# Four edits to an attention and gated-FFN kernel on 8 cores: no casting pre-pass, a layer norm emitted behind the first FFN block, fewer PSUM banks in the projections, an earlier evacuation

## The reference

```python
xn = layernorm(x)                                   # x: [16, 2048, 1024] f32
q, k, v = heads(xn @ Wq + bq), heads(xn @ Wk + bk), heads(xn @ Wv + bv)   # 16 heads of 64
att = softmax(causal(q @ k.T / 8))
y = (att @ v) @ Wo + bo
s = (y - mean(y)) * rsqrt(var(y) + 1e-5) * gamma + beta
wg, wu, wd = w_gate / 127, w_up / 127, w_down / 127  # int32 weights, hidden size 3072
g = silu((silu(xn @ wg.T) * (xn @ wu.T)) @ wd.T)
out = x + s * g
```

## Time and profile before

| what | value |
|---|---|
| median of the 2 runs | 7192.64 us (7139.81 and 7245.48) |
| time of the profiled execution | 7139.81 us |
| its span, slowest core (core 1) | 7138.2 us |
| spans of the 8 cores | 7108.4 to 7138.2 us |
| busy: PE, DVE, ACT, POOL | 81%, 19%, 24%, 1% of the span |
| mean granted TensorE clock | 0.886 on both dies |

### The profile page before, as it was taken

One profiled execution on the slowest core, in us unless ns is written; L12 is line 12 of the kernel. 1 busy time (PEld: TensorE's weight loads), 2 busy tenths in 40 slices (PEclk: granted clock), 3 DMA queues, 4 the chain that ended last, 5 costly groups with the idle time before them and its releaser, 6 DMA issues.

```text
span 7138.2 us, 79504 instructions; the slowest of 8 cores (7108.4 to 7138.2 us)
## 1 busy us (share of the span) xinstructions
PE 5764.5 (81%) x30072; PEld 2865.8 (40%) x30072; DVE 1361.6 (19%) x2330; ACT 1690.2 (24%) x3084; POOL 60.2 (1%) x115
## 2 busy tenths in 40 slices
PE   0158888878788765999999499999999995999998
PEld 0122232233233223766776233333333333766765
DVE  0321121021022014111111311221111114111211
ACT  0413223322322300111111333333333310111111
POOL 0000000000000000000000000000000000000000
PEclk9778888888878777999999688889888887999999
DMA  9630111010110131666666300000000022667666
GB/s 108 209 100 22 31 26 27 25 30 23 27 30 15 28 77 41 152 154 155 154 152 150 116 9 14 14 14 14 12 9 14 5 59 47 152 149 163 155 151 145
DMA packets 1507614, 531.81 MB, mean 75 GB/s; under 512 B 1449766, under 2 KB 1466406, under 8 KB 1506860
## 3 DMA queue, kind: packets, MB, share of 16 engines
q1 hardware_dynamic: 1386172, 402.98, 24.6%
q0 software_dynamic: 13936, 54.53, 4.2%
q10 hardware_dynamic: 107136, 69.22, 3.2%
HBM read 476.29 MB, written 88.08 MB: 79 GB/s over the span
## 4 chain that ended last, share of the span: by engine, by line
PE 74%; DMA 11%; DVE 4%; ACT 4%; issue 3%; SPq 3%; another core or an unknown queue 1%; ACTq 0%; DVEq 0%; POOLq 0%
PE pb L819 15%; PE pb L584 10%; PE pb L1076 9%; PE pb L1064 9%; PE pb L772 8%; PE pb L1140 5%; PE pb L662 5%; DMA pool_b<-scr_wblk 5%; PE pb L943 5%; PE pb L711 3%; SPq L105 3%; DMA pool_f<-x 2%; DMA pool_b<-scr_wraw 2%; DMA scr_wblk<-pool_b 1%; PE pb L781 1%
## 5 line engine op out<-in xcount | busy, mean ns | idle before, releaser
L819 PE MATMUL pb<-pool_f 128*65 128x512 f32 (+3 forms) x2560 | 1158.0, 582 | 0.0
L796 ACT ACTIVATE pool_f<-pb,tiny 128x512 f32<-128x512 f32 (+3 forms) x1280 | 753.1, 622 | 1398.6 <-PE pb L781 922.1
L1064 PE MATMUL pb<-arena_a,pool_b 128*128 128x256 bf16 x6144 | 738.2, 274 | 177.3 <-DMA pool_b<-scr_wblk 172.8
L584 PE MATMUL pb<-arena_a,pool_b 128*128 128x512 bf16 x3072 | 717.9, 393 | 155.1 <-DMA pool_b<-scr_whilo 155.1
L772 PE MATMUL pb<-pool_b 64*128 64x512 bf16 (+3 forms) x3840 | 726.1, 382 | 97.1 <-ACT pool_f L796 97.1
L1140 PE MATMUL pb<-pool_b 128*128 128x512 bf16 x3072 | 692.0, 382 | 109.7 <-DMA pool_b<-scr_wblk 109.0
L1076 PE MATMUL pb<-arena_a,pool_b 128*128 128x256 bf16 x6144 | 734.6, 273 | 11.7 <-ACT pool_f L1153 11.6
L1064 PEld LDWEIGHTS pb<-arena_a,pool_b 128*128 128x128 bf16 x6144 | 601.8, 98 | 257.2 <-issue 185.7
L1076 PEld LDWEIGHTS pb<-arena_a,pool_b 128*128 128x128 bf16 x6144 | 600.5, 98 | 85.8 <-issue 15.4
L819 PEld LDWEIGHTS pb<-pool_f 128*65 128x65 f32 x2560 | 317.7, 147 | 563.5 <-issue 543.4
L584 PEld LDWEIGHTS pb<-arena_a,pool_b 128*128 128x128 bf16 x3072 | 300.0, 101 | 560.9 <-issue 245.1
(11 more groups left out here) (85 smaller groups left out, 2764.3 us busy)
## 6 DMA issues: line engine op xcount, KB each, us to landing
pool_b<-scr_wblk SPq DMA_DIRECT2D x1152, 256.0 KB, 3.4
pool_f<-x SPq DMA_DIRECT2D x96, 512.0 KB, 4.5
pool_b<-scr_whilo SPq DMA_DIRECT2D x96, 256.0 KB, 4.1
pool_b<-scr_wraw POOLq DMA_DIRECT2D x72, 256.0 KB, 2.8
scr_wblk<-pool_b ACTq DMA_DIRECT2D x72, 256.0 KB, 2.6
scr_whilo<-pool_b ACTq DMA_DIRECT2D x64, 256.0 KB, 3.1
scr_o<-pool_b ACTq DMA_DIRECT2D x128, 128.0 KB, 1.8
pool_b<-scr_o SPq DMA_DIRECT2D x64, 256.0 KB, 3.6
```

Of the source, the lines that this page charges most:

```text
L584: e.matmul(o, l, r, start=st, stop=sp)),
L796: e.activation(d, s_, AF.Exp, bias=bc)),
L819: e.matmul(o, l, r, start=st, stop=sp)),
L1064: e.matmul(o, l, r, start=st, stop=sp)),
```

## The change

Four edits go together.

1. The seven casting DMAs and `scr_wraw` are gone. Each unit's load reads 128x1024 int32 elements from the weight itself and casts them to bf16 on the way into SBUF.
2. The K, Q and V projections use PSUM banks `pb[tc % 2]`, and the V transposes `pb[2 + tc % 2]`.
3. `emit_evac` is called when the next query block's scores of `sc == 0` are emitted, not those of `sc == 1`.
4. The first part of an FFN block is a function, `emit_d_p1(tb)`. The first part of block 0 is emitted right behind the output projection, ahead of the layer norm and its fence; the others are called at the end of the block before, which is where they stood. The scratch tiles `sil` and `hfl` move to a part of `pool_f` that the layer norm doesn't use, and the first gate loads wait for the last matmuls of the output projection.

```diff
-    for wi, wsrc in ((0, wg_in), (1, wu_in)):
-        for half in range(2):
-            cast_toks[("gu", wi, half)] = w.dma(
-                "gpsimd", A(scr_wraw, wi * HID * D + half * 1536 * D,
...
-    for g in range(3):
-        cast_toks[("wd", g)] = w.dma(
...
             tok = w.dma("gpsimd", wtl[sl][:, :],
-                        A(scr_wraw, wi * HID * D + hc * 128 * D,
-                          [[D, 128], [1, D]]),
-                        waits=[wblk_state["wtl_cons"][sl],
-                               cast_toks[("gu", wi, hc // 12)]], sem=ld_wt[sl])
+                        A(wsrc, hc * 128 * D, [[D, 128], [1, D]]),
+                        waits=[wblk_state["wtl_cons"][sl]], sem=ld_wt[sl])
...
-                    bank = pb[tc]
+                    bank = pb[tc % 2]
...
-                bankt = pb[tc]
+                bankt = pb[2 + tc % 2]
...
-                    if sc == 1 and evac_pend[0] is not None:
+                    if sc == 0 and evac_pend[0] is not None:
                         emit_evac(*evac_pend[0])
...
         wo_cons0 = [t for ts_ in ofm_slot_cons for t in ts_]
-        suc = statc16[:, 0:16]
...
-        sil = [PF[:, 0:256], PF[:, 256:512]]
-        hfl = [PF[:, 512:768], PF[:, 768:1024]]
+        sil = [PF[:, 6144:6400], PF[:, 6400:6656]]
+        hfl = [PF[:, 6656:6912], PF[:, 6912:7168]]
...
-        for tb in range(8):
+        def emit_d_p1(tb):
...
+            return hi_toks
+
+        wg_cons[0] = wg_cons[0] + wo_cons0
+        wg_cons[1] = wg_cons[1] + wo_cons0
+        hi_toks_next = emit_d_p1(0)
+
+        suc = statc16[:, 0:16]
...
+        w.fence()
+
+        for tb in range(8):
+            hi_toks = hi_toks_next
...
+            if tb < 7:
+                hi_toks_next = emit_d_p1(tb + 1)
```

More of the change, by code:

```diff
@@ L200, in build_program @@
     ld_wt = w.dsem("ld_wt", "gpsimd", 3)
-    ld_cast = w.dsem("ld_cast", "gpsimd", 7)
     st_stg = w.dsem("st_stg", "scalar")
@@ L634, in flush_vtr @@
                                      e.transpose(o, s_, idf_s[:, :])),
-                                    waits=[ev] + pbk_cons[tc], inc=c_te))
-                pbk_cons[tc] = []
+                                    waits=[ev] + pbk_cons[2 + tc % 2], inc=c_te))
+                pbk_cons[2 + tc % 2] = []
                 vfm_cons2[0].append(tks[-1])
@@ L646, in flush_vtr @@
                 v2_cons2[0] = []
-                pbk_cons[tc].append(evv)
+                pbk_cons[2 + tc % 2].append(evv)
                 v2cons.append(evv)
             for tc in range(4):
-                bank = pb[tc]
+                bank = pb[tc % 2]
                 mmt = None
@@ L662, in build_program @@
                                     e.matmul(o, l, r, start=st, stop=sp)),
-                                   waits=[wsl_prod[wn]] + (pbk_cons[tc] if first else []),
+                                   waits=[wsl_prod[wn]] + (pbk_cons[tc % 2] if first else []),
                                    inc=c_te)
@@ L1110, in build_program @@
                 hi_toks.append(l1)
+            return hi_toks
[3 more added lines that the diff above has]
+        suc = statc16[:, 0:16]
+        ssqc = statc16[:, 16:32]
+        negmuc = statc16[:, 32:48]
+        m2c = statc16[:, 48:64]
+        rc16 = statc16[:, 64:80]
+        sq_cons = []
+        stc_toks = []
+        for tt in range(16):
+            yt = s_tile(tt)
+            sq = w.op("scalar", (lambda e, a=yt, tt=tt:
+                                 e.activation(sqc[:, :], a[:, :], AF.Square,
+                                              accum_out=ssqc[:, tt:tt + 1])),
+                      waits=y_cons.get(tt, []) + sq_cons, inc=c_se)
+            sq_cons = [sq]
+            v1 = w.op("vector", (lambda e, a=yt, tt=tt:
+                                 e.reduce_sum(suc[:, tt:tt + 1], a[:, :],
+                                              axis=AX.X)),
+                      waits=y_cons.get(tt, []), inc=c_ve)
+            stc_toks += [sq, v1]
@@ new lines, in build_program @@
+        v3 = w.op("vector", (lambda e: e.tensor_scalar_mul(negmuc, suc,
+                                                           -1.0 / 1024.0)),
+                  waits=stc_toks, inc=c_ve)
+        v4 = w.op("vector", (lambda e: e.tensor_mul(m2c, negmuc, negmuc)),
+                  waits=[v3], inc=c_ve)
+        v5 = w.op("vector", (lambda e: e.scalar_tensor_tensor(
+            m2c, ssqc, 1.0 / 1024.0, m2c, AL.mult, AL.subtract)),
+                  waits=[v4] + stc_toks, inc=c_ve)
+        v5e = w.op("vector", (lambda e: e.tensor_scalar_add(m2c, m2c, 1e-5)),
+                   waits=[v5], inc=c_ve)
@@ new lines, in build_program @@
+        s1 = w.op("scalar", (lambda e: e.activation(rc16, m2c, AF.Ln)),
+                  waits=[v5e], inc=c_se)
+        s2 = w.op("scalar", (lambda e: e.activation(rc16, rc16, AF.Exp,
+                                                    scale=-0.5)),
+                  waits=[s1], inc=c_se)
+        for tt in range(16):
+            yt = s_tile(tt)
+            v6 = w.op("vector", (lambda e, a=yt, tt=tt:
+                                 e.tensor_scalar(a[:, :], a[:, :],
+                                                 negmuc[:, tt:tt + 1],
+                                                 rc16[:, tt:tt + 1],
+                                                 AL.add, AL.mult)),
+                      waits=[s2], inc=c_ve)
+            v7 = w.op("vector", (lambda e, a=yt:
+                                 e.tensor_mul(a[:, :], a[:, :], gamb[:, :])),
+                      waits=[v6, bc_toks[0]], inc=c_ve)
+            v8 = w.op("vector", (lambda e, a=yt:
+                                 e.tensor_add(a[:, :], a[:, :], betb[:, :])),
+                      waits=[v7, bc_toks[1]], inc=c_ve)
+            as_toks.append(v8)
```

27 lines of the change are left out of this document (9 added, 18 removed).

## The result

The changed kernel takes 0.9694 of the time before (95% interval 0.968 to 0.9707); the profiled execution takes 6923.58 us where 7041 was forecast. It is faster by 3.1%, and outside the range given.

A forecast was written before the change was run, and what follows sets the result against it. No single resource was taken as full over the span; each edit was judged by PE's waits at its place. 7139.8 - 164.5 (start) + 61 (casting loads) - 15 (evacuation) + 20 (norm) = 7041.3 us; range 6955 to 7125.

The forecast's parts named there:

- Part 1, the start: At the kernel's start, constants no longer held up by the casts: 164.5 us gained, bias loads done at 12 us.
- The rival of bias loads slow by themselves: At the start, the bias loads' long issue is their own: gain 40 us instead of 164.5, time 7166; chance 0.05.
- Part 1, the casting loads: In the attention of b = 0, casting unit loads take 1.6 us more at each of 38 waits: 61 us lost.
- Part 2, the banks: In the projections and V transposes, using two banks each costs 0, with no projection matmul waiting for DVE.
- Part 3, the evacuation: At the turns between query blocks, evacuating one key block earlier saves 0.3 us, 48 times: 15 us gained.
- The rival of the turn that keeps its clock: At turns between query blocks, PE stays at 2.4 GHz: 108 us gained instead of 15, time 6948; chance 0.12.
- Part 4, the norm: Around the layer norm, its squares start only after the first FFN part's matmuls: 10 us lost per b, 20 in all.

## Why the prediction was wrong

It forecast no change that a measurement can tell, 98 us less, and 219 came (3.1% of 7140). By its own steps:

- **Part 1, the start.** Right in mechanism and size: 164.5 forecast, 168 measured; the constants are complete at 8.9 us, not 12. The rival of bias loads slow by themselves is out.
- **Part 1, the casting loads.** The place and count are right (PE waits for 39 loads, 38 forecast). The load was mis-sized: 1.6 us more was taken, 4.0 against 2.8 is 1.2 measured, and the wait grew by 40.5 us where 61 was forecast. The Trainium skill's fit ("DMA: Bandwidth & Descriptors", "Anatomy of one DMA — SWDGE (gpsimd) path") gave 0.6 more, 23 us, and is about as far off on the other side: it would put the landing at 3.4, and 4.0 was measured. The casts' own rate in the first 177 us gave 4.2 and was the best guide. In the stage the edit costs 38.6 us beside the earlier evacuation and 19.5 alone.
- **Part 2, the banks.** Right: nothing, shown by the run with the banks alone.
- **Part 3, the evacuation.** This step failed. "Mean 0.3 saved for each: 48 x 0.3 = 15 us" should have been 2.3 each, 112 us, shown by the run with this line alone. The idle time of the turn was forecast well (2.5 us; 0.57 + 1.88 = 2.45 measured). The wrong words are "the rest is the same work: at the lower of the two clocks". The same work ran shorter. First, in b = 1, the clock: after the change PE's second broadcast matmul still runs at 2.4 GHz and the stretch at 1.2 GHz is short. The window view shows it, before at the turn of the earlier trace rows and after at the turn shown above (columns as before, the clock third from the end):

```profile
4164.00:4166.00 2.00, 1.35 (x4) 0.71 (x5) 0.00 (x0) 2.00 (x4) 0.00 (x0) 0.85 0.00 0
4166.00:4168.00 2.00, 1.46 (x2) 0.00 (x0) 0.00 (x0) 0.70 (x2) 0.00 (x0) 0.50 0.00 0
...
4172.00:4174.00 2.00, 2.00 (x5) 0.38 (x6) 0.69 (x1) 0.56 (x1) 0.00 (x0) 0.50 0.19 66
4174.00:4176.00 2.00, 2.00 (x8) 0.54 (x5) 0.00 (x0) 0.59 (x2) 0.00 (x0) 0.59 0.19 66
```

```profile
3972.00:3974.00 2.00, 1.76 (x8) 0.52 (x8) 0.68 (x1) 0.62 (x2) 0.00 (x0) 0.92 0.00 0
3974.00:3976.00 2.00, 2.00 (x4) 0.52 (x3) 1.01 (x2) 0.69 (x2) 0.00 (x0) 0.50 0.00 0
3976.00:3978.00 2.00, 2.00 (x8) 0.61 (x7) 0.36 (x1) 1.13 (x2) 0.00 (x0) 0.72 0.38 131
```

  A mean of 0.50 is a slice wholly at the lower level, so the low time is twice what is missing to 1: before 0.6 + 8.0 + 1.6 = 10.2 us (the two slices left out are at 0.50), after 0.3 + 2.0 + 1.1 = 3.4 us. Over all turns of b = 1 the means are 7.9 and, with the evacuation alone, 4.4 us. Why nearly the same idle time lets the clock fall later and rise sooner was not tested. Second, in b = 0 above all, the heads' matmuls: the turn before ran nine and three score matmuls apart. The sum put 0.9 us for six side by side and had the row with 0.80 us for three alone, but did not use it for what it says, that three alone take nearly as long as six. In b = 0 the turn stayed at the lower clock, as the sum had it, and still got shorter by 2.1 us, 1.1 of them in the scores. The rival of the turn that keeps its clock (6948, chance 0.12) named the mechanism of the b = 1 turns, which gained 51 us of the 84 it gave. For b = 0 it gave 24 where 61 came, the largest part of it by the heads' matmuls, which no rival named. The clock rival needed a larger chance, and the low end of the range had to follow it.
- **Part 4, the norm.** Right: 20 us of loss forecast, 16.5 measured, with the idle stretch of 83.1 us where "about 82" stood. That order and fence together are the cause is shown by the run that changed both and removed the stretch.

Put together, the measured terms give the time: the forecast of 7041 less 97 for part 3, less 20 for the casting loads and less some 7 for the start and the norm is 6917, and the stages that should have stood still took 5 more.

What stays open is the clock's own part: which placing of the short waits lets it fall, why the turns of b = 0 stay at 1.2 GHz so much longer than those of b = 1, and why the added waits of the casts give clock back in one kernel and not in the other. Of the 61 us in b = 0, 12 lie outside the turns and were not followed up.

## What to carry to other kernels

Where work is moved across short waits, sum busy and idle time apart, and price the same matmuls at both clock levels: here the idle sum moved by 19 us and the busy sum by 85. Look too at whether matmuls that run side by side are being pulled apart by a wait. Moving an operation past another engine's work hides nothing if all of them share in-order queues and a fence stands behind; emit it piece by piece between the steps it is to hide under. A wait on one count for several slots makes a ring of three buffers a serial chain.

## What the runs showed of the hardware that I had not expected

- A load that casts 512 KB of int32 to 256 KB of bf16 lands in 3.8 to 4.1 us (medians), where the plain 256 KB load took 2.8 and plain 512 KB transfers 3.7 to 5.5. It costs no more than plain transfers of the bytes that it reads.
- Three single-element loads of 1024 descriptors each are complete at 8.9 us when the DMA engines are free, and at 176.5 us when a 38 MB cast fills them; the hold-up shows in the issue times of the SP queue, 0.58 against 52.5 us, as well as in the landing.
- Two groups of three score matmuls on different halves of the rows (64 each) take 0.83 us together at full clock, and one group alone takes 0.80.
- With nearly the same idle time in a turn (2.6 and 2.4 us in the mean of b = 1) the time at 1.2 GHz went from 7.9 to 4.4 us when the waits changed their places.
